# The last MLP of a two-layer decoder on one core: clip factors ahead, maxima by products, four activation buffers, rounding and norm on ScalarE

## The chip, the core and the metric

One core of a Trainium2 chip runs the whole program. The engines are TensorE (PE in the profile, its weight loads PEld), VectorE (DVE), ScalarE (ACT), GpSimd (POOL) and SyncE (SP, which only starts DMAs here). Each runs its instructions in its own order and waits on semaphores. The metric is the device time of one execution in microseconds, as the median of several.

## The reference

The reference is a decoder of two layers on x of 2 x 1024 rows of 256, each sublayer followed by a layer norm. The part that the change touches is the end of it:

```python
def _act_fake_quant(x, clip_factor):
    scale = jax.nn.sigmoid(clip_factor) * jnp.max(jnp.abs(x)) / QMAX
    return jnp.clip(_ste_round(x / scale), -QMAX - 1.0, QMAX) * scale
def _weight_fake_quant(w):
    scale = jnp.max(jnp.abs(w), axis=1, keepdims=True) / QMAX
    return jnp.clip(_ste_round(w / scale), -QMAX - 1.0, QMAX) * scale
xq = _act_fake_quant(x, clip_x[0])
gate = jnp.einsum('bsh,ih->bsi', xq, _weight_fake_quant(w_gate))
up = jnp.einsum('bsh,ih->bsi', xq, _weight_fake_quant(w_up))
h = _act_fake_quant(jax.nn.silu(gate) * up, clip_down[0])
return jnp.einsum('bsi,hi->bsh', h, _weight_fake_quant(w_down))
...
x = _layernorm(x + _L1_xattn_ref(x, ctx_1024, ctx_1024, mask_BxSxS2_bk1, ...), axis=-1)
x = _layernorm(x + _L1_ffn_ref(x, L1_ffn_clip_x, L1_ffn_clip_down, ...), axis=-1)
```

The hidden width is 704. Both scales need a maximum over a whole tensor, of x (2048 x 256) and of the hidden rows (2048 x 704), before anything that follows can be rounded.

## The kernel before

The residual X lies in SBUF as 16 tiles of 128 rows by 256. Each stage is a function per engine (pe_, act_, dve_, pool_, sp_), and the order on each engine is the order in which its functions are written. The change touches two stages.

**The cross attention loop** (pe_l1x, act_l1x, dve_l1x, pool_l1x) runs x = 0 to 23 over the 16 tiles as a software pipeline: scores at x, exponentials x_E at x + 1, their sums at x + 2, POOL's product of x_E with the reciprocals, transposes x_PT at x + 4, the product with the values and the output projection, and VectorE's addition to X (L2148) at x + 7, for two tiles at a time on even x. In x = 10 to 21 the weights of the last MLP are turned by TensorE (L1955, L1958) and copied out by ScalarE (L2062, f_wT and f_dT), through the banks 6 and 7 that the projection also uses. The norm of four tiles at a time is a generator of single VectorE instructions (norm_steps, L230 to L277): four statistics (L237), four aggregations (L242), four small operations on 128x4 numbers in st_r (L246 to L258), three Newton rounds of three small operations (L263, L267, L271) and four normalisings of a tile (L276). norm_and_max adds four maxima of a tile (L2112) into f_am. pump takes so many steps of it in each round of the loop, 9 from x = 7 and all at x = 23; the last four tiles enter at x = 22.

**The last MLP** (pe_l1f, act_l1f, dve_l1f, pool_l1f, sp_l1f):

1. SyncE waits for the last norm and loads the two clip factors into f_cl. ScalarE makes the Exp (L2221), VectorE ends the sigmoid in f_s4 (L2249, L2251), scales the identity by the down weights' scales into f_dg (L2255), TensorE multiplies it with ones so that each row of f_sd holds all of them (L2189's stage begins after it), VectorE copies (L2257).
2. scale_of(.., 0): VectorE reduces the maxima to one per partition, POOL takes the maximum over the partitions (partition_all_reduce, L2330), VectorE makes the scale and its reciprocal in f_s1 (L2264, L2266), then f_sg (L2271).
3. VectorE rounds the 16 tiles of X into three buffers f_Xr in two instructions each (L2276, L2278; adding MAGIC rounds to an integer), TensorE turns them (L2189), ScalarE converts them to bf16 in f_xq (L2224).
4. 24 groups n, each 128 (or 64) hidden rows by 512 columns: g = n // 6, r = n % 6. TensorE makes gate and up into two of eight PSUM banks. ScalarE applies Silu into one of two f_sil (L2234). For even r ScalarE also copies up into f_H (L2237) and POOL multiplies (L2338); for odd r VectorE multiplies straight from PSUM (L2294). VectorE takes each group's maximum, one group later (L2286).
5. scale_of(.., 1) in the same way, with the all-reduce behind POOL's products.
6. Rounding of f_H, six blocks for each g: VectorE five of them in two instructions each (L2307, L2312), POOL block 1 in two (L2343, L2345); ScalarE converts all to bf16 in f_Hq (L2243, L2245), block 1 last.
7. For each of the 16 tiles six products with f_dT into one of four banks, VectorE multiplies by f_sd into one of two f_yt (L2318) and adds to X (L2320), with eight norm steps pumped behind each tile. SyncE writes four tiles out when they are normalised.

The waits that the loop in 4 turns on are these:

```python
                e.wait_ge(s["f_gu"], n + 1)
                if n >= 2:
                    e.wait_ge(s["f_h" if n % 2 else "f_hp"], (n - 2) // 2 + 1)
                e.activation(f_sil[n % 2][0:w, :], PS[0:w, b0, :], ACT.Silu,
```

## Time and profile before

| | us |
|---|---|
| median of 3 runs (2583.32 to 2584.97) | 2584.3 |
| profiled execution | 2585.3 |
| its span | 2583.0 |
| PE busy | 2392.9 |
| DVE busy | 1645.0 |
| ACT busy | 1292.8 |
| POOL busy | 882.5 |
| cross attention ends, maxima of X known | 2466.5 |
| first f_Xr | 2471.42 |
| first Silu | 2484.80 |
| last maximum of the hidden rows begins | 2517.8 |
| first rounding of f_H | 2524.16 |
| first down product | 2540.68 |
| last normalised tile | 2579.57 |

The stage that changes is the last 117 us of 2583. The busy shares of the page are averages over all stages and say nothing on it; here the chain of waits and the order of time are read. A start is in us from the beginning of the span. In the order of time a merged row gives the time from the first start to the last end, and instructions of one engine overlap a little, so that two starts lie closer than one lasts.

### The profile page before, as it was taken

To read this page: it belongs to the slowest core of one execution; us is meant where nothing else is said; L and a number is where in the kernel's file an instruction comes from. 1 tells how busy PE (TensorE), PEld (TensorE's weight loads), DVE (VectorE), ACT (ScalarE), POOL (GpSimd) and SP (SyncE) were. 2 spreads that over 40 slices of the span, in tenths; PEclk is the share of its full clock that TensorE was granted. 3 is DMA by queue.
4 is the path that set the end of the run, shared out by engine and by line. 5 is a ranking of instruction groups with operands and counts; after the bars stand their busy time and mean duration, and the time that the engine had idled before them with its cause. 6 is when DMAs were issued, how large, how long until landed. Compare 5 with 4: busy or idle time off the path is not lost.

```text
span 2583.0 us, 35548 instructions
## 1 busy us (share of the span) xinstructions
PE 2392.9 (93%) x13543; PEld 1709.7 (66%) x13552; DVE 1645.0 (64%) x3008; ACT 1292.8 (50%) x2209; POOL 882.5 (34%) x469
## 2 busy tenths in 40 slices
PE   8999998999999999899999999998899999997763
PEld 7555546755555679788889889897566666555521
DVE  5666754566665566876443443445788888877777
ACT  4565655265555254344444444444266655565742
POOL 3777776176776730202220220301220000302223
PEclk9999999999999999899999999999899999997985
DMA  2001001001000210001100110000434333310000
GB/s 80 13 14 25 13 13 45 13 13 25 13 13 25 90 33 1 33 1 33 34 26 8 33 41 1 9 1 1 108 81 100 88 86 81 85 34 14 1 1 33
DMA packets 55514, 88.11 MB, mean 34 GB/s; under 512 B 11944, under 2 KB 35888, under 8 KB 55344
## 3 DMA queue, kind: packets, MB, share of 16 engines
q1 hardware_dynamic: 55072, 85.70, 12.8%
q8 instruction: 108, 1.77, 0.3%
q14 instruction: 62, 0.51, 0.1%
q10 hardware_dynamic: 272, 0.13, 0.0%
HBM read 37.16 MB, written 2.10 MB: 15 GB/s over the span
## 4 chain that ended last, share of the span: by engine, by line
PE 78%; DVE 11%; ACT 5%; issue 3%; POOL 2%; DMA 1%; SPq 1%; ACTq 0%; another core or an unknown queue 0%; DVEq 0%; POOLq 0%
PE PS L85 76%; DVE m_gl L1237 2%; DVE s_nm L1700 2%; ACT a_P L566 2%; ACT a_QS L515 1%; POOL a_sum L738 1%; ACT x_E L2089 1%; POOL f_H L2338 1%; DVE X L276 1%; DVE st_s L237 1%; DVE s_Zd L1723 0%; DVE s_T L1677 0%; DVE x_sm L2154 0%; PE PS L2189 0%; PE PS L1038 0%
## 5 line engine op out<-in xcount | busy, mean ns | idle before, releaser
L1237 DVE TENSOR_TENSOR m_gl<-m_g,m_gh 128x512 fp32r<-128x512 f32 x288 | 267.0, 933 | 382.7 <-ACT m_g L1099 382.7
L738 POOL TENSOR_TENSOR a_sum<-a_sum,a_P 128x1024 f32<-128x1024 f32 x192 | 456.2, 2376 | 69.4 <-ACT a_P L566 45.6
L566 ACT ACTIVATE a_P<-PS 128x512 f32<-128x512 f32 x512 | 293.7, 600 | 279.9 <-PE PS L85 268.8
L1096 ACT ACTIVATE m_gh<-PS,cols 128x512 fp32r<-128x512 f32 x288 | 198.5, 689 | 464.4 <-PE PS L85 464.4
L613 DVE TENSOR_REDUCE a_nm<-PS 128x1 f32<-128x1024 f32 x256 | 301.5, 1216 | 131.8 <-PE PS L85 130.0
L1700 DVE TENSOR_REDUCE s_nm<-PS 128x1 f32<-128x512 f32 x512 | 331.0, 682 | 76.6 <-PE PS L85 73.9
L85 PE MATMUL PS<-m_w2h,m_gh 128*128 128x256 f32 x1152 | 324.4, 282 | 18.9 <-DVE m_gl L1237 18.7
L85 PE MATMUL PS<-m_w2l,m_gh 128*128 128x256 f32 x1152 | 322.9, 280 | 0.0
L85 PE MATMUL PS<-m_w2h,m_gl 128*128 128x256 f32 x1152 | 322.9, 280 | 0.0
L1598 ACT ACTIVATE s_P<-PS 128x1024 f32<-128x1024 f32 x256 | 248.2, 1022 | 107.6 <-PE PS L85 107.2
L85 PEld LDWEIGHTS PS<-m_w2h,m_gh 128*128 128x128 f32 x1152 | 218.0, 189 | 35.0 <-DVE m_gl L1237 23.4
L85 PE MATMUL PS<-a_P,a_V 128*64 128x512 f32 x1024 | 236.5, 604 | 5.1 <-ACT a_Z L539 5.1
L85 PE MATMUL PS<-xh,m_w1h 128*128 128x512 f32 x576 | 232.6, 404 | 0.0
L85 PE MATMUL PS<-a_QS,a_KH 128*128 128x512 f32 x512 | 221.8, 433 | 10.8 <-ACT a_P L566 8.8
L85 PE MATMUL PS<-xh,m_w1l 128*128 128x512 f32 x576 | 227.4, 395 | 0.0
L85 PE MATMUL PS<-xl,m_w1h 128*128 128x512 f32 x576 | 226.7, 394 | 0.0
L85 PEld LDWEIGHTS PS<-m_w2h,m_gl 128*128 128x128 f32 x1152 | 218.6, 190 | 10.7
L1307 POOL CAST m_w1h<-m_raw 128x2048 fp32r<-128x2048 f32 x9 | 20.0, 2223 | 588.4 <-PE PS L85 587.1
L85 PE MATMUL PS<-s_K,s_Q 128*128 128x512 f32 x512 | 202.3, 449 | 17.8 <-DVE s_nm L1700 8.5
L85 PEld LDWEIGHTS PS<-m_w2l,m_gh 128*128 128x128 f32 x1152 | 218.1, 189 | 0.0
L85 PE MATMUL PS<-a_QM,a_KL 128*128 128x512 f32 x512 | 202.3, 395 | 2.9 <-DMA a_QM<-a_mh 2.9
L1099 ACT ACTIVATE m_g<-PS,cols 128x512 f32<-128x512 f32 x288 | 196.7, 683 | 0.0
(288 smaller groups left out, 4177.6 us busy)
## 6 DMA issues: line engine op xcount, KB each, us to landing
m_raw<-in_m_w SPq DMA_DIRECT2D x16, 1024.0 KB, 5.1
s_Q<-s_T SPq DMA_DIRECT2D x128, 128.0 KB, 2.4
s_K<-s_T SPq DMA_DIRECT2D x128, 128.0 KB, 2.4
a_KH<-a_KH SPq DMA_DIRECT2D x64, 128.0 KB, 2.4
a_wr<-in_w_qk SPq DMA_DIRECT2D x16, 256.0 KB, 2.9
X<-in_x SPq DMA_DIRECT2D x4, 512.0 KB, 6.3
a_P<-in_w_v SPq DMA_DIRECT2D x8, 256.0 KB, 5.8
m_raw<-in_c_w SPq DMA_DIRECT2D x2, 1024.0 KB, 8.9
```

What stands on the lines that cost most here:

```text
L85: return e.matmul(o, l, r, start=start, stop=stop, skip_group_check=shared)
L237: e.bn_stats(st_s[:, j, :], X[:, j, :]).then_inc(own.sem, 1)
L276: e.tensor_scalar(X[:, j, :], X[:, j, :], st_a[:, j, 0:1], st_r[:, 0, j:j + 1], ALU.subtract, ALU.mult).then_inc(s["normed"], 1)
L515: ins = e.activation(QS[i][a][R[a], cs], PS[R[a], bk, :], ACT.Copy, scale=0.125)
L566: e.activation(a_P[:, g % N_P, half * 512:half * 512 + 512], PS[:, s0 + half, :], ACT.Exp).then_inc(s["a_exp"], 1)
L613: e.tensor_reduce(a_nm[:, n % 2, 8 * a + i:8 * a + i + 1], PS[:, bk:bk + 2, :], AX.XY, ALU.max, negate=True).then_inc(s["a_max"], 1)
L738: e.tensor_tensor(o[:, :], a_P[:, (g - 1) % N_P, :] if k == 1 else o[:, :], a_P[:, g % N_P, :], ALU.add).then_inc(s["a_add"], 1)
L1096: e.activation(m_gh[r][:, :], PS[:, 4 + n % 3, :], func, bias=cols[:, bcol:bcol + 1]).then_inc(s["m_gh"], 1)
L1099: e.activation(m_g0[r][:, :], PS[:, 4 + n % 3, :], func, bias=cols[:, bcol:bcol + 1]).then_inc(s["m_g0"], 1)
L1237: e.tensor_tensor(m_gl[r][:, :], m_g0[r][:, :], m_gh[r][:, :].bitcast(F32), ALU.subtract).then_inc(s["m_gl"], 1)
L1598: e.activation(s_P[w % 4][:, :].rearrange("p (a n) -> p a n", a=2), PS[:, bk:bk + 2, :], ACT.Exp, scale=0.25).then_inc(s["s_exp"], 1)
L1700: e.tensor_reduce(nm2[:, n % 2, i, half:half + 1], PS[:, bank["natural", z], :], AX.X, ALU.max, negate=True).then_inc(s["s_nr"], 1)
```

## The change

In the loop of the cross attention: at x = 18 ScalarE makes the Exp of the clip factors and VectorE the two diagonals f_dg; at x = 19 TensorE multiplies them with ones; at x = 20 VectorE copies f_sd and ends the sigmoid; at x = 23 ScalarE makes a Silu of the two clip factors, whose output isn't used. VectorE pumps all steps of the norm from x = 18 on, not from x = 23. SyncE loads the clip factors without waiting for the norm.

In the last MLP: the maximum over the partitions is taken by scaling the identity with the maxima (f_dm), one product with ones, which puts all 128 on every partition, and a reduction from PSUM. There are four f_sil, and ScalarE's wait goes back four groups. POOL no longer rounds: ScalarE scales the blocks 1, 2, 4 and 5 and adds MAGIC in one activation, VectorE clamps the sum in one instruction; VectorE rounds blocks 0 and 3 in two as before; ScalarE converts all six. VectorE rounds groups 0 and 1, then evacuates the first four tiles, rounds group 2, evacuates four tiles, rounds group 3. POOL adds the evacuated tiles (in four buffers) to X. VectorE computes only the statistics, the scale and the bias of the norm, and ScalarE applies them.

```diff
             for x in range(N_C):
...
+                if x == 19:
+                    e.wait_ge(s["x_ex"], NT)
+                    e.wait_ge(s["f_dv"], 2)
+                    for k in range(2):
+                        t = mm(e, PS[:, 2, k * 128:(k + 1) * 128], ones[:, :], f_dg[:, k, :], True, True)
+                    t.then_inc(s["f_sp"], 1)
...
+                if x == 18:
+                    e.wait_ge(s["f_cl"], 16)
+                    e.activation(f_s4[:, :], f_cl[:, :], ACT.Exp, scale=-1.0).then_inc(s["f_e4"], 1)
+                if x == N_C - 1:
+                    e.activation(f_si[:, :], f_cl[:, :], ACT.Silu)
...
-                pump(slow, 12 if x < 7 else 9 if x < N_C - 1 else 99)
+                pump(slow, 12 if x < 7 else 9 if x < NT + 2 else 99)
...
+            def maxima(k, bk):
+                e.wait_ge(s["f_dm"], k + 1)
+                mm(e, PS[:, bk, 0:128], ones[:, :], f_dm[:, :], True, True).then_inc(s["f_sp"], 1)
...
-                if n >= 2:
-                    e.wait_ge(s["f_h" if n % 2 else "f_hp"], (n - 2) // 2 + 1)
-                e.activation(f_sil[n % 2][0:w, :], PS[0:w, b0, :], ACT.Silu,
+                if n >= 4:
+                    e.wait_ge(s["f_h" if n % 2 else "f_hp"], (n - 4) // 2 + 1)
+                e.activation(f_sil[n % 4][0:w, :], PS[0:w, b0, :], ACT.Silu,
...
+            def scaled(g, r):
+                h = f_H[0:IR[r], r, g * 512:g * 512 + 512]
+                e.activation(h, h, ACT.Copy, scale=f_s1[0:IR[r], 7:8], bias=MAGIC).then_inc(s["f_ha"], 1)
...
+            def normal(g):
+                e.wait_ge(s["f_nb"], g + 1)
+                for j in range(4 * g, 4 * g + 4):
+                    e.activation(X[:, j, :], X[:, j, :], ACT.Identity, bias=st_r[:, 1, j:j + 1],
+                                 scale=st_r[:, 0, j:j + 1]).then_inc(s["f_out"], 1)
...
-                e.tensor_reduce(f_s1[:, o:o + 1], amax, AX.X, ALU.max).then_inc(s["f_sm"], 1)
-                e.wait_ge(s["f_par"], k + 1)
-                e.wait_ge(own.sem, s4)
+                e.tensor_reduce(f_s1[:, o:o + 1], amax, AX.X, ALU.max).then_inc(own.sem, 1)
+                e.wait_ge(own.sem, own.up())
+                e.tensor_scalar(f_dm[:, :], ident[:, :], f_s1[:, o:o + 1], None, ALU.mult).then_inc(s["f_dm"], 1)
+                e.wait_ge(s["f_sp"], k + 2)
+                e.tensor_reduce(f_s1[:, o + 1:o + 2], PS[:, bk, 0:128], AX.X, ALU.max).then_inc(own.sem, 1)
...
-            for j in range(NT):
-                e.wait_ge(s["f_yp"], j + 1)
-                e.tensor_tensor(f_yt[j % 2][:, :], PS[:, 2 * (j % 4), 0:256], f_sd[:, :], ALU.mult).then_inc(s["f_y"], 1)
-                e.wait_ge(s["f_y"], j + 1)
-                e.tensor_tensor(X[:, j, :], X[:, j, :], f_yt[j % 2][:, :], ALU.add).then_inc(s["f_res"], 1)
-                pump(slow, 8)
...
+            for g in range(4):
+                for j in range(4 * g, 4 * g + 4):
+                    e.wait_ge(s["f_yp"], j + 1)
+                    if j >= 4:
+                        e.wait_ge(s["f_res"], j - 3)
+                    e.tensor_tensor(f_yt[j % 4][:, :], PS[:, 2 * (j % 4), 0:256], f_sd[:, :], ALU.mult).then_inc(s["f_y"], 1)
+                    pump(slow, 3)
+                if g < 2:
+                    for _ in rounded(g + 2):
+                        pump(slow, 2)
+                slow.append(norm_part(g))
             pump(slow, 99)
...
+            for j in range(NT):
+                e.wait_ge(s["f_y"], j + 1)
+                e.tensor_tensor(X[:, j, :], X[:, j, :], f_yt[j % 4][:, :], ALU.add).then_inc(s["f_res"], 1)
```

On POOL, at the end of the program of before, L2330 is the all-reduce and the rows called ISA without operands are configuration instructions that the compiler adds:

```order
256 L2330 ISA
257 L2330 ISA f_s1<-f_s1 128x1 [waits f_sm]
258 L2338 ISA
259 L2338 TENSOR_TENSOR f_H<-f_H,f_sil0 128x512 [waits f_up] x12
260 L2330 ISA
261 L2330 ISA f_s1<-f_s1 128x1 [waits f_sm]
262 L2343 ISA
263 L2343 TENSOR_SCALAR f_H<-f_H,f_s1 128x512 [waits f_s1]
264 L2345 TENSOR_SCALAR f_H<-f_H 128x512 [waits f_hpr]
```

Now POOL has in this place, numbers left out, only the products and then the additions (f_Xr is the tensor that f_yt shares):

```order
236 L2193 TENSOR_TENSOR x_E<-x_E,x_rd 128x1024 [waits x_rcp] x16
237 L2390 TENSOR_TENSOR f_H<-f_H,f_sil 128x512 [waits f_up] x12
238 L2393 TENSOR_TENSOR X<-X,f_Xr 128x256 [waits f_y] x16
239 L76 UNCONDITIONAL_BRANCH
```

The two all-reduces, their three changes of configuration and the eight roundings are gone, and sixteen additions came.

On VectorE, in the middle of the down products (the second norm beside tiles 10 to 13), before has in a row:

```order
1855 L2318 TENSOR_TENSOR f_yt<-PS,f_sd 128x256 [waits f_yp]
1856 L2320 TENSOR_TENSOR X<-X,f_yt 128x256 [waits f_y]
1857 L246 TENSOR_SCALAR st_r<-st_a 128x4 [waits dve]
1858 L250 TENSOR_SCALAR st_r<-st_r 128x4 [waits dve]
1859 L254 TENSOR_SCALAR st_r<-st_r 128x4 [waits dve]
1860 L258 TENSOR_SCALAR st_r<-st_r 128x4 [waits dve]
1861 L263 TENSOR_TENSOR st_r<-st_r 128x4 [waits dve]
1862 L267 TENSOR_TENSOR st_r<-st_r 128x4 [waits dve]
```

and now, from tile 10 on:

```order
1847 L2377 TENSOR_TENSOR f_Xr<-PS,f_sd 128x256 [waits f_res,f_yp]
1848 L241 BN_AGGR st_a<-st_s 128x2 [waits dve] x2
1849 L245 TENSOR_SCALAR st_r<-st_a 128x4 [waits dve]
1850 L2377 TENSOR_TENSOR f_Xr<-PS,f_sd 128x256 [waits f_res,f_yp]
1851 L249 TENSOR_SCALAR st_r<-st_r 128x4 [waits dve]
1852 L253 TENSOR_SCALAR st_r<-st_r 128x4 [waits dve]
1853 L257 TENSOR_SCALAR st_r<-st_r 128x4 [waits dve]
1854 L2377 TENSOR_TENSOR f_Xr<-PS,f_sd 128x256 [waits f_res,f_yp]
```

The addition behind each evacuation has left VectorE, and three small steps of the norm stand between two evacuations.

On ScalarE, from the end of the loop ahead to the first groups, before has:

```order
1623 L2221 ACTIVATE f_s<-f_cl 128x2 [waits f_cl]
1624 L2224 ACTIVATE f_xq<-PS 128x2x256 [waits f_xt] x8
1625 L2234 ACT_TABLE_LOAD [waits f_gu]
1626 L2234 ACTIVATE f_sil<-PS,f_sg 128x512 [waits f_dv]
1627 L2237 ACTIVATE f_H<-PS,f_sg 128x512
1628 L2234 ACTIVATE f_sil<-PS,f_sg 128x512 [waits f_gu]
```

and now:

```order
1625 L2115 ACTIVATE f_si<-f_cl 128x2
1626 L2252 ACTIVATE f_xq<-PS 128x2x256 [waits f_xt] x8
1627 L2262 ACTIVATE f_sil<-PS,f_sg 128x512 [waits f_gu,f_dv]
1628 L2265 ACTIVATE f_H<-PS,f_sg 128x512
1629 L2262 ACTIVATE f_sil<-PS,f_sg 128x512 [waits f_gu] x2
```

The table load stands ahead of f_si, in the loop's last round, and none follows it.

## Rows read from the trace of the kernel before

**Rows 1.** Chain of waits, 2455 to 2583: start us, us, what
```profile
2468.57 1.24 PE PS L85 x4
...
2483.50 1.28 ACT L2234
...
2493.51 0.69 ACT f_H L2237
2494.27 1.28 POOL f_H L2338
...
2496.22 0.69 ACT f_H L2237
...
2518.70 4.65 issue
```

**Rows 2.** VectorE and ScalarE in order of time; in brackets the idle time before and its releaser
```profile
2454.32 0.42 DVE L2148 TENSOR_TENSOR X<-PS,X 128x256 f32<-128x256 f32 x1 [3.13 <-PE PS L85]
2467.73 0.20 ACT L2221 ACTIVATE f_s<-f_cl 128x2 f32<-128x2 f32 x1 [10.95 <-DMA f_cl<-in_f_clip]
```

**Rows 3.** VectorE: maxima of X (ns min/median/max, first and last start), what follows, PSUM evacuations
```profile
L2112 DVE TENSOR_REDUCE f_am<-X x8: 406/408/409, 2457.4 to 2466.1; 128x1 f32<-128x256 f32 x8
2471.42 0.35 DVE L2276 TENSOR_SCALAR f_Xr<-X,f_s 128x256 f32<-128x256 f32 x1
2518.52 0.18 DVE L2261 TENSOR_REDUCE f_s<-f_am 128x1 f32<-128x24 f32 x1
L2318 DVE TENSOR_TENSOR f_yt<-PS,f_sd 128x256 f32<-128x256 f32 x16 | 6.6, 414 | 2.6 <-PE PS L85 2.6
```

**Rows 4.** The gate and up loop in order of time; one stretch: length, five engines' busy time, PEclk
```profile
2483.21 0.15 PEld L85 LDWEIGHTS PS<-f_xq,f_wT 128*128 128x128 bf16 x1 [0.28 <-issue]
2484.49 2.56 PEld L85 LDWEIGHTS PS<-f_xq,f_wT 128*128 128x128 bf16 x12 [0.28 <-issue]
2485.38 0.68 ACT L2237 ACTIVATE f_H<-PS,f_sg 128x512 f32<-128x512 f32 x1
2487.46 1.28 DVE L2286 TENSOR_REDUCE f_am<-f_H 128x1 f32<-128x512 f32 x2
2489.40 0.75 DVE L2294 SCALAR_TENSOR_TENSOR f_H<-PS,f_sg,f_sil 128x512 f32<-128x512 f32 x1 [0.66 <-ACT f_sil L2234]
2485.00:2517.00 32.00, 22.21 (x87) 7.08 (x86) 22.79 (x34) 21.88 (x36) 15.04 (x12) 0.97 0.00 1
```

**Rows 5.** POOL's roundings behind the second all-reduce; the same in ns min/median/max
```profile
2530.95 4.60 POOL L2343 TENSOR_SCALAR f_H<-f_H,f_s 128x512 f32<-128x512 f32 x1 [7.22 <-issue]
L2343 POOL TENSOR_SCALAR f_H<-f_H,f_s x4: 2002/2152/4597, 2531.0 to 2548.6; 128x512 f32<-128x512 f32 x4
```

**Rows 6.** Rounding and conversions, ScalarE's copies from PSUM, one stretch of the down products
```profile
2524.16 0.88 DVE L2307 TENSOR_SCALAR f_H<-f_H,f_s 128x512 f32<-128x512 f32 x2
2540.53 2.69 ACT L2243 ACTIVATE f_Hq<-f_H 128x512 bf16<-128x512 f32 x5
L2224 ACT ACTIVATE f_xq<-PS 128x512 bf16<-128x512 f32 x8 | 4.8, 598 | 9.6 <-PE PS L2189 9.6
2540.70:2546.30 5.60, 5.60 (x24) 2.67 (x24) 3.17 (x8) 4.67 (x10) 5.42 (x3) 0.52 0.00 0
```

**Rows 7.** POOL's product of x_E and VectorE's small steps beside POOL; POOL's additions of 128x256
```profile
2360.30 1.90 POOL L2166 TENSOR_TENSOR x_E<-x_E,x_rd 128x1024 f32<-128x1024 f32 x1 [5.84 <-DVE x_rd L2136]
2360.42 1.80 DVE L246 TENSOR_SCALAR st_r<-st_a 128x4 f32<-128x4 f32 x1
2550.75 0.57 DVE L246 TENSOR_SCALAR st_r<-st_a 128x4 f32<-128x4 f32 x1
L1321 POOL TENSOR_TENSOR X<-X,rows x16: 733/742/1198, 892.7 to 927.0; 128x256 f32<-128x256 f32 x16
```

**Rows 8.** VectorE at the end: last statistics, last normalisings
```profile
2573.75 1.40 DVE L237 BATCH_NORM_STATS2 st_s<-X 128x6 f32<-128x256 f32 x4
2578.18 1.38 DVE L276 TENSOR_SCALAR X<-X,st_a,st_r 128x256 f32<-128x256 f32 x4
```

More of the change, by code:

```diff
@@ L226, in program, with norm_scales @@
         ov = out.rearrange("(t p) d -> p t d", p=128)
-        def norm_steps(e, own, tiles, waits):
+        def norm_scales(e, own, tiles, waits):
             lo, hi = tiles[0], tiles[-1] + 1
@@ L273, in norm_steps @@
                 yield
+            return t
+        def norm_steps(e, own, tiles, waits):
+            t = yield from norm_scales(e, own, tiles, waits)
             for j in tiles:
@@ L2208, in pe_l1f @@
                 t.then_inc(s["f_gu"], 1)
+            maxima(1, 7)
             for j in range(NT):
@@ L2219, in act_l1f @@
         def act_l1f(e):
-            e.wait_ge(s["f_cl"], 16)
-            e.activation(f_s4[:, :], f_cl[:, :], ACT.Exp, scale=-1.0).then_inc(s["f_e4"], 1)
             for j in range(1, NT, 2):
@@ new lines, in norm_part @@
+            def norm_part(g):
+                tiles = range(4 * g, 4 * g + 4)
+                t = yield from norm_scales(e, own, tiles, {j: (s["f_res"], j + 1) for j in tiles})
+                e.wait_ge(own.sem, t)
+                e.scalar_tensor_tensor(st_r[:, 1, 4 * g:4 * g + 4], st_a[:, 4 * g:4 * g + 4, 0], -1.0,
+                                       st_r[:, 0, 4 * g:4 * g + 4], ALU.mult, ALU.mult).then_inc(s["f_nb"], 1)
+                yield
+            slow = []
+            for g in range(2):
+                pump([rounded(g)], 99)
```

128 lines of the change are left out of this document (61 added, 67 removed).

## The prediction

> **What bounds the kernel now.** The diff touches the last MLP and a little of the loop ahead of it, so first the chain of waits from 2455 us on, then the order of time of each engine in the same stretch, then the granted clock by stretches. Four pieces are not arithmetic: the clip factors arrive by a DMA and an Exp only when the maxima are known [rows 2]; ScalarE loads a table of 1.28 us with TensorE's first group already done [rows 1]; after the last maximum of the hidden rows nothing runs for 4.65 us ahead of the second all-reduce [rows 1]; and POOL stands 7.22 us before it rounds block 1 [rows 5], for which the down products wait until about 2540.7 [rows 6]. Between them lies the gate and up loop, whose period is ScalarE's copy, POOL's product, ScalarE's Silu, in turn, because two Silu buffers are reused. After 2540.7 the VectorE queue sets the end: evacuation, addition and norm of 16 tiles, up to 2579.57 [rows 8].
>
> I follow one moment at a time through the new order. The profiled span is 2583.0 and its execution 2585.3; the median of the runs is 2584.3, so 1.3 us is added to a span.
>
> **1. The end of the loop ahead.** Two products with ones go onto TensorE at x = 19, an Exp of 0.20 onto ScalarE at x = 18 [rows 2], 0.5 us of diagonals onto VectorE at x = 18, and the copy and two small operations at x = 20, where VectorE next waits for TensorE. What is queued behind the two products is a turn of the down weights and its copy, which the next product waits for. In the kernel before the two took 1.24 us [rows 1]; a part hides under ScalarE, which is full there. On VectorE the norm of tiles 8 to 11 is now pumped to its end at x = 19: its last three Newton operations, four normalisings and four maxima, some 3.2 us, move into a wait of 3.13 us for TensorE [rows 2]. Together with the diagonals they overrun it by some 0.5 us, and the last two additions no longer start back to back but when TensorE ends. Bounds -0.1 (all hidden) and +1.2; I take +0.4, nearer to the wait that swallows most of it. The Silu load falls into x = 23, where ScalarE has 10.95 us of nothing [rows 2]. The clip DMA is started early, past no other transfer.
>
> **2. The first scale.** The last maximum of X ends at 2466.1 + 0.41 = 2466.5 and the first f_Xr starts at 2471.42: 4.9 us [rows 3]. New: reduction 0.20, diagonal 0.25 (two in 0.46), one product, reduction from PSUM, two small operations 0.40, f_sg 0.15. The product: two took 1.24, so one lies between 0.62 and 1.24; I take 0.70, as the start is paid once. A PSUM reduction of 128 columns lies between 0.18 (24 columns from SBUF) and 0.42 (256 evacuated) [rows 3]; 0.35, for PSUM. Sum 2.05. With part 1, f_Xr starts at 2466.5 + 0.4 + 2.05 = 2468.95: **-2.5**.
>
> **3. Into the gate and up loop.** The transposes keep their pace (three f_Xr are still cycled). The load of 1.28 goes, the first Silu comes at 2481.0. TensorE's first weight loads start 0.43 us apart (three from 2483.21 to 2484.49), 512 columns at 1.2 GHz [rows 4]; the second group ends at about 2485.0 in the old count, 2482.5 now, and with a Silu as long as the copies, 0.69, VectorE's first product starts at 2483.3.
>
> **4. The loop.** A pair of blocks takes 2.71 us now, from copy to copy: 0.69 and a gap of 0.07, the product's 1.28, and the 0.67 to the Silu's end [rows 1]. With four Silu buffers each engine is left with its own work per pair: ScalarE three activations, 1.75 (0.58 each: the 0.68 of the rows less an overlap of 0.10); POOL 1.27; TensorE 8 x 0.213 (12 in 2.56) = 1.7 at the granted clock of 0.97 [rows 4]; VectorE 0.75 for the product and two reductions that end 1.28 after the first starts, of which the next product overlaps 0.07, 1.96. VectorE is the bound, with 0.2 us in hand. 12 x 1.96 = 23.5, so the last maximum ends at 2506.8 where it was 2518.5 [rows 3]: **-11.7** in all. Bounds for a pair: 1.93 and 2.1.
>
> **5. The second scale.** From there to the rounding were 5.64 us; part 2's sum without f_sg is 1.95, and the rounding starts at 2508.8 where it was 2524.16 [rows 6]: **-15.3** in all. The program of before holds extra configuration rows on POOL around each all-reduce, and the gaps named "issue", 4.65 in the chain and 7.22 on POOL, stand exactly there [rows 1, 5]; the new one has none.
>
> **6. Rounding to the end**, counted from T = 2508.8. ScalarE has per 512 columns four scaled rows and six conversions. A conversion is 0.52 (five in 2.69) [rows 6]; a scaled row has a column as scale, which from PSUM cost 0.08 more than without [rows 4, 6], so 0.59. One group is 5.5 us, ready at T+5.5 and T+11.0. TensorE starts cold: 24 products, four tiles, took 5.6 us and their last drain at a granted clock of 0.52 [rows 6], so with 1.5 a tile tile 3 ends at T+11.5 and its evacuation at T+12.0. Only then comes VectorE's rounding of group 2: four operations in 1.46 (two in 0.88 less an overlap, and two that don't read a column), during which POOL's additions may take 0.75, while ScalarE stands since T+12.1 for row 0. It goes on at T+14.0, and after two conversions and two scaled rows and a last clamp VectorE is free for tile 4 at T+16.6. From here VectorE's queue never empties: 12 evacuations x 0.45 (0.41 [rows 3] and the gap) = 5.4; group 3's eight operations 2.8; four norms of 4.55 (some 4.35 in before's last one, statistics to normalising [rows 8], and 0.2 for the bias) = 18.2. That makes T+43.0.
>
> Then the ports. While POOL multiplies x_E, the next small operation of VectorE on st_r doesn't take 0.17 but lasts until POOL's end: 1.80 beside a POOL instruction of 1.90, both ending at 2362.2 [rows 7]. Statistics and reductions aren't held. In the new order tiles 6, 7 and 10 to 14, seven in all, have such small steps right behind an addition that POOL has just begun, and POOL's 128x256 additions take 0.74 [rows 7]. Each holds VectorE for about 0.7: +4.9. Against it speaks one row: beside a later rounding of POOL's, of 2 us [rows 5], the first small step took 0.57 [rows 7], but that is an operation with one tensor. Bounds 0 and 7 x 1.2 = 8.4 (the longest row of that shape, 1.198); I take 4.9, by the rows with two tensors. So f_nb of the last group is at T+47.9. ScalarE ends the norm: a 128x256 activation without columns starts 0.3 after the last, one of 512 columns with one 0.58; I take 0.47, and 0.05 + 4 x 0.47 + 0.1 = 2.0 for four. T+49.9 = 2558.7. The transfer and its end took 2583.0 - 2579.57 = 3.43 [rows 8]. Span 2562.1, time **2563.5** (-0.8%).
>
> The Trainium skill, page "SBUF — State Buffer", section "Who interferes with whom", calls the pair of ports that VectorE and GpSimd share an exclusive lock held for a whole instruction, taken by VectorE's tensor_scalar in a fast mode and by operations with two SBUF inputs; the rows of x_E agree. By it the sum would be the 2563.5 above; without it, rival A's 2558. The page "ScalarE: Activation LUTs", section "What ACT_TABLE_LOAD costs", gives some 93 ns for each column operand; by it a normalising activation starts 0.49 after the last, the sum +0.1; no row here shows one with two columns.
>
> **The rivals.** A, no hold: POOL's small additions don't stop VectorE, as in the row of 0.57. Price -4.9, less 0.7 in group 2: 2558. B, the loop doesn't do what it says: something else still paces the pair at 2.71, as the in-order wait of ScalarE for the product four rows back behind a late POOL. ScalarE's 1.75 and POOL's 1.27 leave room, which speaks against it. 12 x 0.75 = 9.0: 2572.5. C, the clock: TensorE starts at 1.2 GHz and is granted 0.97 in the loop [rows 4]. If it stays at 1.2 GHz, a pair takes 8 x 0.427 = 3.4: 12 x 1.46 = 17.5, 2581. The loop is denser than before, when the clock rose, which speaks against it. D, starved additions: POOL's first rounding took 4.60 beside VectorE's chained tensor_scalar, others 2.0 [rows 5]. At that ratio an addition takes 1.7, every tile waits for it, and 12 us come on top: 2575. E, **slower than before**: the same mechanism at its full price. 4.60 for 512 columns are 2.3 for the 256 of an addition. Then evacuation, addition and small steps go one after another: T+10 to the first, 16 x 2.3 = 36.8, the roundings of groups 2 and 3 between them with their waits for ScalarE 14, two norms 9.1, ScalarE 2.0: T+72, against the T+71 at which the gain is gone. From 2.3 us per addition on it decides; at 2.5 the time is 2588.
>
> **How the numbers follow.** Forecast 0.62, A 0.20, B 0.05, C 0.04, D 0.07, E 0.02. The forecast's own errors (product 0.62 to 1.24 twice, pair 1.93 to 2.1, scaled row 0.52 to 0.69, holds 0 to 8.4) span 2557 to 2569; the range takes in A, and leaves out C, E and most of B and D: 2556 to 2570. Some 0.2% (5 us) is what a measurement can tell from no change. Faster by more: all but C and E, with a little for errors: 0.93; within: 0.05; slower: 0.02.
>
> **What would show it.** A Silu period of 1.96 with VectorE never idle in the loop; no table load after 2460; some 2 us from the last maximum to each scale, with no gap on POOL; ScalarE's first six conversions done 5.5 us after the scale, and a stall of about 2 us ahead of row 0 of group 2; VectorE's small steps of 0.6 to 0.8 us beside POOL's additions seven times; two norms at the end with nothing between. It is wrong where the conversions of the last group, not VectorE, end last, where a pair is over 2.1 us, or where the stretch from scale to end is under 46 or over 54 us.

## The result, and where the time went

The changed kernel takes **2555.0 us** (median of 4 runs, 2551.8 to 2557.4) against 2583.8 for the kernel before beside it (median of 4, 2578.4 to 2585.0): ratio 0.9892, 95% interval 0.9873 to 0.9910. The forecast was 2563.5 with a range from 2556 to 2570. The direction and the order of the gains were right, but the kernel is 8.5 us faster than the forecast and 1.0 us faster than the range allowed. The profiled execution has a span of 2555.6 and took 2557.4.

Not all of a difference between two executions belongs to a change. The addition of tile 11 in the loop ahead (start 2447.05 in the kernel before, 2445.35 now) stands ahead of everything that changed on the five engines but the transfer of the clip factors, which now starts at 2327.4, and in the fourteen executions below it lies anywhere from 2439.1 to 2446.9. I call it the **anchor**, and compare stretches that begin there. From anchor to end the kernel before takes 135.95 us, the changed one 110.25, and a second execution of the changed one 110.25 again: **25.7 us** gained. The medians differ by 28.8 here and by 26.5 in the second measurement. What goes beyond 25.7 isn't shown to be the change's.

VectorE and ScalarE of the changed kernel from the last maxima of X to the first Silu; start, duration, engine and line, in brackets the idle time before and its releaser:

```profile
2463.54 1.39 DVE L2126 TENSOR_REDUCE f_am<-X 128x1 f32<-128x256 f32 x4
2466.34 0.29 DVE L2303 TENSOR_REDUCE f_s<-PS 128x1 f32<-128x128 f32 x1 [0.89 <-PE PS L85]
2466.86 0.16 DVE L2307 RECIPROCAL f_s<-f_s 128x1 f32<-128x1 f32 x1
2479.28 0.69 ACT L2262 ACTIVATE f_sil<-PS,f_sg 128x512 f32<-128x512 f32 x1 [1.17 <-PE PS L85]
```

The maxima end at 2464.93, the first scaled row starts at 2467.20. That is 2.27 us where [rows 3] gave 4.92, and no row of the clip factors is left in between. The first Silu has no table load ahead of it.

The gate and up loop, VectorE; then one stretch of all engines (length, then busy time with instructions of TensorE, its weight loads, VectorE, ScalarE, POOL, then the granted clock, DMA share, GB/s):

```profile
2481.24 0.75 DVE L2335 SCALAR_TENSOR_TENSOR f_H<-PS,f_sg,f_sil 128x512 f32<-128x512 f32 x1 [4.47 <-ACT f_sil L2262]
...
2494.19 0.73 DVE L2335 SCALAR_TENSOR_TENSOR f_H<-PS,f_sg,f_sil 128x512 f32<-128x512 f32 x1
2494.85 1.26 DVE L2327 TENSOR_REDUCE f_am<-f_H 128x1 f32<-128x512 f32 x2
2496.04 0.73 DVE L2335 SCALAR_TENSOR_TENSOR f_H<-PS,f_sg,f_sil 64x512 f32<-64x512 f32 x1
...
2502.23 1.26 DVE L2327 TENSOR_REDUCE f_am<-f_H 128x1 f32<-128x512 f32 x2
```
```profile
2481.00:2504.00 23.00, 18.90 (x84) 7.65 (x82) 22.70 (x38) 19.48 (x34) 14.89 (x12) 0.98 0.00 1
```

From product to product are 1.85 us (2494.19 to 2496.04) where [rows 1] gave 2.71, and from its first product at 2481.24 on VectorE never stands: 22.70 busy in 23.00. The product is recorded with 0.73, but its successor starts 0.66 behind it.

The stretch from the second scale to the end, four engines; ScalarE's stalls, the evacuations of tiles 3, 4, 8, 12 and 15, two scalings with small steps between them, and one small step beside an addition of POOL. T is the second scale, the moment at which the rounding may start, here 2505.62:

```profile
2505.62 1.33 ACT L2270 ACTIVATE f_H<-f_H,f_s 128x512 f32<-128x512 f32 x2 [4.78 <-DVE f_s L2307]
2517.32 0.42 DVE L2377 TENSOR_TENSOR f_Xr<-PS,f_sd 128x256 f32<-128x256 f32 x1 [0.67 <-PE PS L85]
2519.69 0.63 ACT L2275 ACTIVATE f_Hq<-f_H 128x512 bf16<-128x512 f32 x1 [1.57 <-DVE f_H L2352]
2522.44 0.41 DVE L2377 TENSOR_TENSOR f_Xr<-PS,f_sd 128x256 f32<-128x256 f32 x1
2527.18 0.48 DVE L2347 TENSOR_SCALAR f_H<-f_H,f_s 128x512 f32<-128x512 f32 x1
2527.84 0.48 DVE L2347 TENSOR_SCALAR f_H<-f_H,f_s 128x512 f32<-128x512 f32 x1
2528.96 0.63 ACT L2275 ACTIVATE f_Hq<-f_H 128x512 bf16<-128x512 f32 x1 [3.59 <-DVE f_H L2352]
2531.71 0.41 DVE L2377 TENSOR_TENSOR f_Xr<-PS,f_sd 128x256 f32<-128x256 f32 x1
2536.45 0.42 DVE L2377 TENSOR_TENSOR f_Xr<-PS,f_sd 128x256 f32<-128x256 f32 x1
2536.95 0.72 POOL L2393 TENSOR_TENSOR X<-X,f_Xr 128x256 f32<-128x256 f32 x1 [0.64 <-DVE f_Xr L2377]
2536.79 0.15 DVE L262 TENSOR_TENSOR st_r<-st_r 128x4 f32<-128x4 f32 x1
2536.97 0.72 DVE L266 TENSOR_TENSOR st_r<-st_r 128x4 f32<-128x4 f32 x1
2537.72 0.16 DVE L270 SCALAR_TENSOR_TENSOR st_r<-st_r 128x4 f32<-128x4 f32 x1
2540.52 0.42 DVE L2377 TENSOR_TENSOR f_Xr<-PS,f_sd 128x256 f32<-128x256 f32 x1
2549.87 0.16 DVE L2363 SCALAR_TENSOR_TENSOR st_r<-st_a,st_r 128x4 f32<-128x4 f32 x1
2550.07 2.07 ACT L2280 ACTIVATE X<-X,st_r 128x256 f32<-128x256 f32 x4 [2.44 <-DVE st_r L2363]
```

L266 takes 0.72 us and ends with POOL's addition. L262, 0.18 earlier, had slipped in ahead of the addition. The same operations take 0.16 when POOL is idle. The evacuation at 2536.45 is recorded with 0.42, but the next operation starts 0.34 behind it.

Counted from the anchor, or from the moment before; the two rows on the norm both count from T:

| step | before | forecast | after |
|---|---|---|---|
| anchor to the last maximum of X | 19.45 | 19.85 | 19.58 |
| to the first scaled row | 4.92 | 2.05 | 2.27 |
| to the first Silu | 13.38 | 12.1 | 12.08 |
| to VectorE's first product | 1.95 | 2.3 | 1.96 |
| to the last maximum of the hidden rows | 31.7 | 23.5 | 22.25 |
| to the second scale | 5.7 | 1.95 | 2.13 |
| to VectorE's last step of the norm | | 47.9 | 44.4 |
| to ScalarE's end (before: VectorE's) | 55.4 | 49.9 | 46.5 |
| to the end of the span | 3.43 | 3.43 | 3.46 |

### The profile page after: what moved, and what is told of

The parts are those of the page before. It is cut to its first block, busy times and chain, and to the rows that moved or that the text cites. A ratio compares the mean times of both kernels' runs of the same rounds, so it can differ in the third digit from the quotient of the medians.

```text
span 2555.6 us, 35564 instructions
## 1 busy us (share of the span) xinstructions
PE 2392.2 (94%) x13547; PEld 1711.0 (67%) x13556; DVE 1630.6 (64%) x2976; ACT 1309.9 (51%) x2242; POOL 872.4 (34%) x475
## 4 chain that ended last, share of the span: by engine, by line
PE 79%; DVE 11%; ACT 6%; issue 2%; POOL 1%; DMA 1%; SPq 1%; ACTq 0%; another core or an unknown queue 0%; DVEq 0%; POOLq 0%
PE PS L85 77%; DVE m_gl L1240 2%; DVE s_nm L1703 2%; ACT a_P L569 2%; ACT a_QS L518 1%; POOL a_sum L741 1%; ACT x_E L2098 1%; DVE f_am L2327 1%; DVE st_s L236 1%; DVE s_T L1680 0%; DVE x_sm L2168 0%; PE PS L2220 0%; DVE X L279 0%; DVE s_Zd L1726 0%; PE PS L1041 0%
```

## The experiments

Each is one execution, with its stretches read from the anchor on, unless a ratio stands with it.

**Two Silu buffers instead of four.**

```diff
-f_sil = [sb(c, f"f_sil{i}", [128, 512]) for i in range(4)]
+f_sil = [sb(c, f"f_sil{i}", [128, 512]) for i in range(2)]
-                if n >= 4:
-                    e.wait_ge(s["f_h" if n % 2 else "f_hp"], (n - 4) // 2 + 1)
+                if n >= 2:
+                    e.wait_ge(s["f_h" if n % 2 else "f_hp"], (n - 2) // 2 + 1)
```

> The changed kernel with two Silu buffers instead of four and nothing else; the Silu waits for the product two blocks back again. Theory (the reuse of a buffer ties copy, product and Silu into one ring): a pair of blocks takes the 2.71 us of before instead of 1.85, 12 pairs cost 12 x 0.86 = 10.3 us, and the last maximum of the hidden rows ends 10 us later after the first Silu than in the changed kernel (32.5 instead of 22.2). Rival (the slow pair of before came from its other parts, as POOL set up for its all-reduce between the products): the pair stays at 1.85 and the time at that of the changed kernel.

ScalarE at the third Silu, and VectorE's last two pairs of maxima:

```profile
2480.16 0.69 ACT L2262 ACTIVATE f_sil<-PS,f_sg 128x512 f32<-128x512 f32 x1 [0.87 <-POOL f_H L2390]
...
2507.14 1.28 DVE L2327 TENSOR_REDUCE f_am<-f_H 128x1 f32<-128x512 f32 x2
2509.84 1.27 DVE L2327 TENSOR_REDUCE f_am<-f_H 128x1 f32<-128x512 f32 x2
```

The pair is back at 2.70 and the Silu waits for POOL's product. The loop takes 31.70 us, which is the kernel before's 31.73; the stretch from the anchor is 119.7, so 9.4 more. I had multiplied by twelve pairs. Between the first product and the last maximum lie eleven periods and one pair's own length: 11 x 0.86 = 9.5. Of the 25.7 us gained, the buffers alone carry 9.4, the largest single part.

**One more reduction per pair.**

```diff
                 if n:
                     maximum(n - 1)
+                    if n % 2 == 0:
+                        e.wait_ge(s["f_h"], n // 2)
+                        e.tensor_reduce(f_s1[0:IR[(n - 1) % 6], 8:9], <the same block>, AX.X, ALU.max, ...)
```

> The changed kernel with one more reduction on VectorE in each of 11 pairs of the gate and up loop: the maximum of the odd block is taken a second time, into a column that nobody reads. Theory (VectorE sets the pair of 1.85 us, and a reduction behind another costs its pitch of 0.60): 11 x 0.60 = 6.6, the loop from the first product to the last maximum is 28.9 us instead of 22.25. Rival (ScalarE's three activations, 1.73 with their pitch, or TensorE set the pair, and VectorE has room): only what exceeds that room, below 5 us; at twice the pitch forecast from single rows, 0.67 or more, over 7.3.

```profile
2500.07 1.26 DVE L2327 TENSOR_REDUCE f_am<-f_H 128x1 f32<-128x512 f32 x2
2501.25 0.67 DVE L2341 TENSOR_REDUCE f_s<-f_H 128x1 f32<-128x512 f32 x1
2501.84 0.73 DVE L2335 SCALAR_TENSOR_TENSOR f_H<-PS,f_sg,f_sil 64x512 f32<-64x512 f32 x1
```

The loop is 28.76, so 6.51 / 11 = 0.59 for an operation recorded with 0.67. Two things follow: VectorE is the bound with no room left, and a queued instruction starts 0.07 to 0.09 before the recorded end of the one before it. I call the distance from one start to the next the **pitch**. A period is the sum of these pitches, 0.66 + 0.59 + 0.60 = 1.85.

**The preparation of the clip factors alone**, put into the kernel before:

```diff
+                if x == 19:      # TensorE: the two products with ones
+                if x == 18:      # ScalarE: Exp; VectorE: the diagonals
+                if x == 20:      # VectorE: copy, two small operations
...
-                pump(slow, 12 if x < 7 else 9 if x < N_C - 1 else 99)
+                pump(slow, 12 if x < 7 else 9 if x < NT + 2 else 99)
```

> The kernel before with the preparation of the clip factors in the loop ahead, and nothing else of the change: both all-reduces, two Silu buffers and POOL's rounding stay. Theory (the first scale waited for this preparation alone, the all-reduce is quick there): from the last maximum of X to the first scaled row 1.4 us where it was 4.92, and every later moment of the chain 3.4 us earlier, so the time is 3.4 us less than before; the loop ahead is longer by 0.1. Rival (the all-reduce was getting ready behind that work): the 4.9 us stay and the time is that of before.

VectorE after the first all-reduce, and POOL at the second:

```profile
2463.36 0.16 DVE L2267 TENSOR_TENSOR f_s<-f_s 128x1 f32<-128x1 f32 x1 [0.55 <-POOL f_s L2333]
2463.90 0.35 DVE L2279 TENSOR_SCALAR f_Xr<-X,f_s 128x256 f32<-128x256 f32 x1
```
```profile
2508.35 1.26 POOL L2341 TENSOR_TENSOR f_H<-f_H,f_sil 128x512 f32<-128x512 f32 x1 [1.44 <-ACT f_H L2252]
2515.65 0.38 POOL L2333 PARTITION_ALL_REDUCE f_s<-f_s  x1 [6.04 <-issue]
```

From the last maximum of X to the scaled row 1.29 instead of 4.92; from anchor to end 132.38, that is 3.57 less than before. What the first scale had waited for was this preparation, and the first all-reduce was never slow (0.55 of VectorE's time).

**POOL's all-reduce for the first maximum, and for the second.**

```diff
+            def across(i, k):
+                e.wait_ge(s["f_sm"], i + 1)
+                e.partition_all_reduce(f_s1[:, 4*k+1:4*k+2], f_s1[:, 4*k:4*k+1], 128, ...max).then_inc(s["f_par"], 1)
+            across(0, 0)      # the one kernel: ahead of POOL's products
...
+            across(0, 1)      # the other: behind them
```

> The changed kernel with POOL's all-reduce for the maximum of X, as before the change; the hidden rows' maximum keeps the product with ones. Theory (the first all-reduce was quick in the kernel before, some 0.54 us between the operations on either side of it, since POOL had long stood idle): from the last maximum of X to the first scaled row 0.20 + 0.54 + 0.40 + 0.17 and small gaps, 1.4 us, against 2.27 with the product; 0.9 us faster. Rival (an all-reduce always brings the 4.65 us of nothing that stood ahead of the second one): 5.5 us and more, 3 us slower.

> The changed kernel with POOL's all-reduce for the maximum of the hidden rows, as before the change, and the product with ones for the maximum of X. Theory (an all-reduce is slow when POOL has just run its products): 5.5 us from the last maximum to the first rounding instead of 2.13, so 3.4 us slower. Rival (only the second all-reduce of a kernel is slow, whatever stands before it): with one all-reduce alone 1.2 us, 1.0 us faster.

The first kernel's VectorE, and TensorE's clock at its entry into the loop; the second kernel's POOL:

```profile
2464.28 0.16 DVE L2319 TENSOR_TENSOR f_s<-f_s 128x1 f32<-128x1 f32 x1 [0.55 <-POOL f_s L2402]
2464.82 0.35 DVE L2331 TENSOR_SCALAR f_Xr<-X,f_s 128x256 f32<-128x256 f32 x1
```
```profile
2476.00:2478.00 2.00, 2.00 (x6) 0.73 (x5) 0.00 (x0) 1.10 (x2) 0.00 (x0) 0.50 0.00 0
2478.00:2480.00 2.00, 2.00 (x11) 0.91 (x10) 0.84 (x2) 1.63 (x4) 1.27 (x1) 1.00 0.00 0
```
```profile
2498.39 1.26 POOL L2409 TENSOR_TENSOR f_H<-f_H,f_sil 128x512 f32<-128x512 f32 x1 [0.46 <-ACT f_H L2269]
2505.43 0.38 POOL L2402 PARTITION_ALL_REDUCE f_s<-f_s  x1 [5.78 <-issue]
```

For the first maximum the all-reduce takes 1.29 us against 2.27, so here the product with ones **costs** 0.98. Only 0.5 of that reaches the end: the clock goes from 1.2 to 2.4 GHz (0.50 to 1.00 in the rows) 34.1 us behind the anchor as in the changed kernel (34.0), though all work comes 1.0 us earlier. So it rises 1.1 us behind the first Silu, where it had done so at the Silu, VectorE's first product comes 0.3 later and the loop takes 0.2 more. For the second maximum the scale takes 4.75 against 2.13, 2.6 us slower. It is this kernel's only all-reduce, so the rival doesn't hold. That is the theory's sign, with less than its 3.4: the all-reduce begins 5.8 to 6.2 us after POOL's last product in all three kernels (the kernel before, the one above and this one), and since VectorE now sets the loop, POOL is done with its products 1.8 us ahead of the last maximum, where it was 1.3.

The profile dates POOL's change of configuration for the second all-reduce 5.8 to 6.0 us ahead of it in these three kernels (2517.4 in the kernel before, for 2523.36), and for the first one 24 us ahead (2446.7 for 2470.5). That fits a change of configuration of some 6 us which runs unseen where POOL is idle for long enough, but no run shows it apart from the product that stands before it.

**Without the early Silu.**

```diff
-                if x == N_C - 1:
-                    e.activation(f_si[:, :], f_cl[:, :], ACT.Silu)
```

> The changed kernel without the Silu at the end of the loop ahead, whose only use is to bring its table. Theory (the load of 1.28 us then falls behind the wait for TensorE's first group, where all wait for it): 13.4 us from the first scaled row to the first Silu instead of 12.1. Rival (ScalarE stands 1.17 us idle ahead of its first Silu, and the load finds room there): 12.1 to 12.2, no cost.

```profile
2474.73 1.28 ACT L2260 ACT_TABLE_LOAD   x1 [1.15 <-PE PS L85]
```

The load stands behind the 1.15 us of waiting for TensorE's group, not in it: 13.36 us to the first Silu, 1.28 more, and the end 1.2 later.

**The additions on VectorE.**

```diff
                     e.tensor_tensor(f_yt[j % 4][:, :], PS[:, 2 * (j % 4), 0:256], f_sd[:, :], ALU.mult).then_inc(s["f_y"], 1)
+                    e.wait_ge(s["f_y"], j + 1)
+                    e.tensor_tensor(X[:, j, :], X[:, j, :], f_yt[j % 4][:, :], ALU.add).then_inc(s["f_res"], 1)
                     pump(slow, 3)
```

> The changed kernel with the 16 additions of the residual on VectorE, each right behind its evacuation, and nothing on POOL after the gate and up loop. Theory (POOL's additions hold VectorE's small steps): the small steps that took 0.64 to 0.72 us now take 0.16 like all others, which gives back 3.8 us, and 16 additions of some 0.35 cost 5.6; the stretch from the second scale to the last small step is 44.4 + 1.8 = 46.2 us. Rival (a small step behind an evacuation is slow by itself): the rows of 0.7 stay, and the stretch is 50.

```profile
2535.34 0.42 DVE L2379 TENSOR_TENSOR X<-X,f_Xr 128x256 f32<-128x256 f32 x1
2535.68 0.15 DVE L262 TENSOR_TENSOR st_r<-st_r 128x4 f32<-128x4 f32 x1
2535.87 0.16 DVE L266 TENSOR_TENSOR st_r<-st_r 128x4 f32<-128x4 f32 x1
```

All seven held steps are back at 0.16 to 0.17, and the last one ends at T+46.6, 2.2 later. So the hold is POOL's doing. It costs 5 x 0.56 and 2 x 0.48, together 3.8 us, for 12 additions that cost VectorE some 0.46 each here (0.80 for an evacuation and its addition, 0.34 for an evacuation). The Trainium skill, page "SBUF — State Buffer", section "Who interferes with whom", says that whichever of the two issues first has the shared ports for the whole instruction. The held step agrees: L266 started 0.02 behind POOL's addition and took 0.72, as long as that. L262 had just ended when the addition started, so these rows don't show VectorE holding POOL.

**VectorE rounds all rows.**

```diff
-                for r in (0, 3):                        # in rounded(g): two operations each
+                for rs in ((0, 3), (1, 2), (4, 5)):     # all six rows
...
-                scaled(g, 1)                            # ScalarE: four scaled copies a group
+                for r in DONE:                          # conversions alone
```

> The changed kernel with ScalarE's scaled copies undone: VectorE scales and rounds all six rows of a group with two operations each, 12 operations at 4.4 us a group, and ScalarE only converts. Theory (early on VectorE stood waiting for ScalarE, so the extra work there is free): the first group is ready at T+5.0 instead of T+5.6 (T is the second scale), the tile of y 4 is evacuated at T+15.9 instead of T+16.8, and only in the third and fourth group do the extra four operations cost 1.6 us each; the last small step ends at T+45.1 where it was T+44.4. Rival (VectorE is the bound from the scale on, so that what ScalarE took off it is all gained): 16 more operations at 0.37 and more, T+50.

The last step ends at T+45.4, 1.0 us later than in the changed kernel, with sixteen more operations on VectorE. The theory holds: most of what ScalarE took over had been free. The tile of y 4 comes at T+16.6, not at 15.9.

**VectorE's own roundings earlier.**

```diff
+            def clamped(g): ...      # the clamps behind ScalarE's scaled copies, out of rounded(g)
-            for g in range(2):
-                pump([rounded(g)], 99)
+            pump([rounded(0)], 99)
+            for g, own_rows in ((0, [rounded(1)]), (1, [rounded(2), rounded(3)])):
+                for _ in clamped(g):
+                    pump(own_rows, g + 1)
```

> The changed kernel with VectorE's own eight roundings of groups 2 and 3 (two blocks, two operations each) moved forward into the 3.4 us in which it waits for ScalarE's scaled blocks of groups 0 and 1. Theory (VectorE's queue after the tile of y 3 sets the end, and what leaves it is gained whole): ScalarE no longer stalls 1.57 and 3.59 us for these blocks, tile 4 is evacuated 1.4 us earlier, at T+15.4, and the last small step ends 3 us earlier, at T+41.4. Rival (the moved operations delay the clamps for which ScalarE waits at the start, and the gain goes there): T+44.

```profile
2517.94 2.94 DVE L2361 TENSOR_SCALAR f_H<-f_H 128x512 f32<-128x512 f32 x4
2520.80 0.41 DVE L2384 TENSOR_TENSOR f_Xr<-PS,f_sd 128x256 f32<-128x256 f32 x1
```

Tile 4 is evacuated at T+15.2 and the last step ends at T+41.2: 3.2 us less, as expected. The queue of VectorE is what ends last.

**Statistics behind the evacuations, small steps for eight tiles.**

```diff
+                    if j >= 10:
+                        slow.append(stats([j - 2]))
+                    if j >= 4:
+                        pump(slow, 2)
+                if g == 1:
+                    slow += [stats(range(4, 8)), scales(0, 8)]
...
-                slow.append(norm_part(g))
+            slow += [stats((14, 15)), scales(8, 16)]
```

> The changed kernel with another order of the last norm: behind an evacuation stand the statistics of the tile two before, which POOL's additions did not hold in any row, and no small steps; the small steps are taken for eight tiles at once, so two sets of 14 instead of four. Theory (a small step on two tensors is held by POOL's addition, statistics are not): no row of 0.6 to 0.7 us for a small step; evacuations 8 to 15 pass at about 0.79 us a tile, two sets of steps (2.8 us each) are saved, four more normalising activations stand at the end (+2.0): ScalarE ends at T+40.5 instead of T+46.5. Rival (statistics are held as well once they stand there, or the additions come late and everything waits for them): 8 x 0.35 more, T+43.3 and above.

POOL's first five additions of the second half, and a statistic of VectorE among them:

```profile
2534.58 3.46 POOL L2413 TENSOR_TENSOR X<-X,f_Xr 128x256 f32<-128x256 f32 x5 [7.37 <-DVE f_Xr L2390]
```
```profile
2536.23 0.42 DVE L2363 BATCH_NORM_STATS2 st_s<-X 128x6 f32<-128x256 f32 x1
```

No small step is held and no statistic is (0.42 beside POOL, as without). ScalarE ends at T+42.25, 4.3 us earlier, not 6: an aggregation behind each statistic makes a tile 0.87 long, where I had 0.79, and two tiles come 0.28 and 0.13 late, the first of them with a wait for TensorE. That is about 1 us of the 1.75; the rest isn't split up.

**Together, and the last transfers apart.** The four edits with a gain in one kernel, VectorE normalising tiles 13 to 15; then the same with tiles 10, 11 and 15:

```diff
-            for j in (13, 14, 15):
+            for j in (10, 11, 15):
...
-                e.wait_ge(s["f_out"], min(4 * g + 4, 13))
+                e.wait_ge(s["f_out"], (4, 8, 10, 13)[g])
```

> Four things together on the changed kernel: POOL's all-reduce for the first maximum (1.0 us less to the first scaled row), VectorE's own roundings of groups 2 and 3 moved into its waits (3.2 us less), the norm with statistics behind the evacuations and small steps for eight tiles at once (4.3 us less), and the last three of the sixteen tiles normalised by VectorE while ScalarE does the five before. Theory (the gains lie one behind the other on VectorE's queue and add): the stretch from the second scale to the last normalising is 36.3 us instead of 46.5, the first scale gives 0.5 to 1.0 more, so the time is 11 us under the changed kernel's. Rival (with VectorE's queue shorter, the down products, which need ScalarE's conversions, become the bound): group 3's conversions end 22.4 us after the scale, the tiles 12 to 15 are evacuated not before T+28, and the stretch is 39 us or more; 7 us under.

> The changed kernel as it is, on the same chip and in the same rounds as the combination of edits, so that the two can be set side by side. Its stretches from the addition of tile 11 on should repeat to 0.3 us: 19.6 to the last maximum of X, 2.3 to the first scaled row, 12.1 to the first Silu, 22.25 for the loop, 2.13 for the second scale, 44.4 to the last small step. The start of the last stretch moves by some us between executions, the ratio to the kernel before should be 0.989.

> The same combination a second time, five more runs. The stretch from the addition of tile 11 to the end repeats 102.3 us to 0.3. If what lies ahead of it is noise, the median is some 8 us under the 2555 of the changed kernel, about 2547; if the combination lengthens it, as its first runs may be read, 2551 again.

> The combination of edits with VectorE's three normalisings moved: tiles 10, 11 and 15 instead of 13, 14 and 15, so that tiles 8 to 11 can leave 1 us earlier. Theory (the last two output transfers of 0.5 MB each ran one behind the other at 345 GB/s, and the last one waited for the first): from the last normalising to the end 3.5 us instead of 4.5, the stretch from the addition of tile 11 to the end 101.3 us instead of 102.3 (changed kernel 110.25). Rival (the longer end is that of any transfer issued right behind another, however far its predecessor has come): 4.5, no gain. In the times 9 us under the changed kernel's 2555 if the start of the stretch is noise, 5 us if the new code itself moves it.

Tiles 12 to 15 in the combination's first and second execution; the third number from the end is the granted clock:

```profile
2536.00:2538.00 2.00, 1.15 (x8) 0.59 (x7) 1.86 (x8) 0.00 (x0) 1.57 (x3) 1.00 0.79 269
```
```profile
2535.50:2537.50 2.00, 2.00 (x10) 0.79 (x7) 1.19 (x5) 0.00 (x0) 1.22 (x2) 0.50 0.81 269
```

The end of the combination and of the kernel with the transfers apart; the last two numbers are the DMA share and GB/s:

```profile
2546.00:2548.00 2.00, 0.00 (x0) 0.00 (x0) 0.00 (x0) 0.00 (x0) 0.00 (x0) 0.50 1.04 345
```
```profile
2542.00:2544.00 2.00, 0.00 (x0) 0.00 (x0) 0.00 (x0) 0.00 (x0) 0.00 (x0) 0.50 0.84 292
```

| kernel | median us | ratio to before | 95% interval | anchor to end |
|---|---|---|---|---|
| changed, first and second time | 2555.0, 2555.4 | 0.9892, 0.9900 | 0.9873 to 0.9910, 0.9886 to 0.9913 | 110.25, 110.25 |
| combination, first and second time | 2551.1, 2548.9 | 0.9880, 0.9872 | 0.9866 to 0.9894, 0.9857 to 0.9886 | 102.3, 103.4 |
| with the transfers apart | **2545.8** | **0.9855** | 0.9839 to 0.9872 | 102.4 |

The combination's stretch from T to ScalarE's end is 38.0, near the rival's 39. VectorE comes to tile 8 only at T+25.0, because aggregations and steps still stand ahead of the clamps. The second time it was 39.2, so the stretch did not repeat to 0.3 as expected: TensorE stayed at 1.2 GHz through tiles 12 to 15 (granted clock 0.50, where the first time it was 1.00 from 2536 on) and made VectorE wait 0.53 for each of the last two tiles. With the transfers apart, the end behind the last normalising is 3.5 us instead of 4.5, as its theory said. In the combination the last two transfers of 0.5 MB start 0.55 us apart (2544.25 and 2544.80), and the last one lands 4.0 us after its start where an output transfer otherwise takes 2.9. Here they start 1.5 apart and the last one is not late, nor is it in the run with the statistics behind the evacuations, where they start 2.0 apart. This execution too stayed at 1.2 GHz, with the same two waits of 0.53, so it is to be set against the combination's second one: 102.4 against 103.4.

Of the gain of 8 us from the anchor on, the first run of the combination showed 4.3 in its medians, the second 6.5 (both against 2555.4; from the anchor on 8.0 and 6.8). The last kernel shows 9.6 against the changed one, with 7.9 from the anchor on. So the medians lie between 3.7 us under and 1.7 over what the anchored stretches give. The 2440 us ahead move by as much without any change: the changed kernel's own anchor is at 2445.35 in one execution and at 2442.35 in the other, with a granted clock of 0.97 between 800 and 1200 us in the first and 0.98 in the second. Of all sixteen traces four show 0.98 there, with anchors from 2439.1 to 2442.35, and twelve show 0.97, with anchors from 2440.8 to 2447.05. That fits a clock that differs from one execution to the next. Whether anything of a kernel's own code takes part in it isn't settled.

## Why the prediction fell short, point by point

The step that failed is the price of VectorE's full queue, in parts 4 and 6. The prediction added recorded durations, with an overlap once a pair and a gap behind each evacuation, and a held step at its full length. The runs showed smaller distances from start to start: 1.845 us a pair instead of 1.96, 0.34 an evacuation instead of 0.45, and 3.8 us for the seven holds instead of 4.9. The loop took 22.25 instead of 23.5 and the stretch from T to the last small step 44.4 instead of 47.9.

- **The end of the loop ahead (+0.4):** +0.1. The overrun of 0.5 is there: the addition of tile 12 comes 7.77 us behind the anchor where it came 7.27. But ahead of tile 14 VectorE waits another 2.08 us for TensorE, where before it ran without a wait, and all but 0.1 vanishes in that. The value lay near the lower bound of the prediction, "all hidden".
- **The first scale (2.05):** 2.27, the one term that was too low. The product with its way back took 0.89 of VectorE's idle time, where the sum had 0.70; the reduction, the small operations and the diagonal came within 0.04 of the list. That this step gained at all was no merit of the product with ones: 3.6 us of the old 4.9 were the preparation, and the all-reduce was 1.0 faster than its replacement.
- **Into the loop (the load's 1.3, first product 2.3 behind the Silu):** 1.30, confirmed by the run without the early Silu (1.28); the product came at 1.96, as before. I had let TensorE's 1.2 GHz delay the second group, but the clock rose at the first Silu.
- **The loop (pair 1.96, bounds 1.93 to 2.1):** the bound was named rightly and sized wrongly, 1.845. What failed here is "0.75 for the product and two reductions that end 1.28 after the first starts, of which the next product overlaps 0.07": the overlap was granted once a pair, but each of the three has it. Eleven periods and their tail: -1.25 us. Both ends of my bounds lay above the value, so the range was too narrow here.
- **The second scale (1.95):** 2.13, again the product's way. That the gap named "issue" goes with the all-reduce was right: it came back with it.
- **Rounding to the end (47.9 to the last small step):** 44.4, the largest miss, -3.5. Its beginning was right to 0.2 us: tile 3 was evacuated at T+12.1 (12.0), tile 4 came at T+16.8 (16.6); ScalarE's stall was 1.57 (about 2). The second stall of 3.59, ahead of group 3, it did not list. The holds were right in number, seven, and in kind. They cost 3.8, not 4.9, since only what exceeds the step's own 0.16 is lost, and that was in the norms already: -1.1. The other 2.4 are pitches once more. An evacuation in a full queue takes 0.34 instead of 0.45, twelve times, -1.3. In the norms that run between other work, a small step costs about 0.14 where alone it has a pitch of 0.20, as two of them between two scalings show (0.66 from one scaling to the next, less 0.39 for the scaling itself). To that I put down the remaining -1.1; this is argued, no run shows it apart. A norm with nothing between took 4.51 from its first statistic to the next norm's (4.55).
- **ScalarE ends the norm (2.0), the last transfer (3.43):** 2.1 and 3.46. The normalising activations start 0.49 apart: four took 2.07, with 0.60 for the last. The forecast's 0.47 was 0.1 low in the sum. The Trainium skill's figure for a column operand (page "ScalarE: Activation LUTs", section "What ACT_TABLE_LOAD costs") gave an estimate of 0.49, and the trace agrees with it.

Together these make -4.8 of the 8.5 us. Another 1.7 is the earlier anchor in the profiled execution, and the rest lies between that execution and the median of four: 2557.4 against 2555.0, with 1.8 instead of 1.3 outside the span. The 4.8 alone would have given 2558.7, inside the range. That the time left it is in part chance: the kernel's own steps account for little more than half of the miss.

**The rivals.** A, no hold, gave 2558 and stood nearer to the measured time than the forecast, but only by luck. It is wrong: the rows of 0.72 and the run with the additions on VectorE show the hold. B's mechanism is what two buffers give; with four, nothing else paced the pair. C did not come: 0.98. D and E did not: an addition took 0.72 to 0.74.

## What to carry to other kernels

Price a queue that never runs empty by the distance from start to start, not by recorded durations: those of VectorE's large operations were 0.07 to 0.09 us longer than their pitch, and some fifty of them made about half of the 4.8 us by which the stretch from the anchor on was forecast too long. Before moving work between engines, look who waits: sixteen operations taken off VectorE were worth 1.0 us, since it stood waiting there, and moving eight within its own queue was worth 3.2. When two kernels differ by a few us in thousands, anchor both traces at the last instruction ahead of the change; such stretches repeated to 0.1 us where the clock rose at the same point, and differed by 1.1 where it did not, while whole runs of one kernel scattered by 5 and more.

## What the runs showed of the hardware

- POOL's all-reduce of one column takes 0.38 us, and 0.55 of VectorE's time, when POOL has been idle for 20 us or more, but starts 5.8 to 6.2 us after POOL's last product of two tensors. The replacement by a product with ones pays only there (-2.6); for the first maximum it costs 1.0, of which 0.5 reaches the end.
- Of two small operations right behind an evacuation, the first slips in before POOL's addition and the second is held to its end, whether it has one input tensor (L253, 0.72) or two (L266, 0.72). Statistics (0.42) are not held. Two scalings of 512 columns beside POOL's additions took 1.66 together, where they take 0.88.
- In all fifteen traces with the new loop ahead TensorE's granted clock rises from 0.50 to 1.00 between 33.7 and 34.2 us behind the anchor (in the kernel before, 37.6), whether the first Silu comes at 33.0 (first all-reduce) or at 35.2 (without the early Silu). So the chain that the first all-reduce moved forward by 1 us did not bring the faster clock forward. Near the end the same code ran tiles 14 and 15 at 2.4 GHz in one execution and at 1.2 GHz in another, which cost 1.1 us.
- Two output transfers of 0.5 MB issued 0.55 us apart ran together at 345 GB/s, and the last one landed 1.0 us later for it. Issued 1.5 or 2.0 us apart, the last one was not late.
